# Mamba block with an FP4 feed-forward on one core: TensorE sums all sixteen products of a unit

## Chip, cores, metric

The kernel runs on one core of one Trainium2 chip. The metric is the device time of one execution in microseconds (us); less is better. Engines carry the names of the profile: PE is TensorE's matmul, PEld its weight load, DVE is VectorE, ACT is ScalarE, POOL is GpSimd, SP is SyncE.

## What is computed

An input of 16 sequences of 1024 tokens with 256 features goes through two residual layers, all in f32. The first is a state space layer with 4 heads of 128 channels, the second a gated feed-forward layer of width 704 whose activations and weights are rounded to blocks of FP4. The part that the change touches is the readout of the state space layer:

```
def step(s, inp):
    d_t, u_t, B_t, C_t = inp
    dA = jnp.exp(d_t[..., None] * A)
    s = s * dA + (d_t * u_t)[..., None] * B_t[:, :, None, :]
    y_t = jnp.einsum('bhdn,bhn->bhd', s, C_t)
    return (s, y_t)
```

The state has 16 entries n for each channel. y_t is the sum over these 16 of state times C.

## The kernel before

**Units and steps.** A unit is 512 tokens of one head; there are 128 units. A unit has 16 steps, one for each state entry n. At step n VectorE scans the 512 tokens of entry n in one instruction (L888), after it has multiplied the next entry's input term in PSUM (L878). Units 0 to 3 of each group of 8 are the first halves of a sequence for the four heads ("early" units here), units 4 to 7 the second halves ("late" units). After the last scan of an early unit VectorE copies the last column of the 16 states into carry (L893), which the late unit's scans start from. There is no such copy in a late unit.

**Readout.** Entries are taken in pairs p = 0 to 7. For a pair GpSimd multiplies two states with two rows of C into one of the four slots of prod (L619, 128 x 1024). For the pairs in the tuple ADDED, which are 0, 2, 4 and 6, GpSimd then adds the two halves of that slot (L623, 128 x 512). TensorE sums the products of a unit into the PSUM tensor ybank with an identity matrix as weights (L951, in sum_up): one f32 matmul of 512 columns for an added pair, two for any other. So a unit has 12 of these matmuls. Each f32 matmul shows in the profile as two records, its two passes. When the eighth pair is in, VectorE takes ybank into yg (L749).

**The order of the work is written out by hand.** Each engine has a function step(b, j, n) that is unrolled for the 8 units of a batch and 16 steps each; the batches 1 to 14 are a loop, the first and the last are peeled, with 8 units of lead and 8 of trail. The other work of both layers is laid into these steps: timetable gives for each job its unit, and due(job, slot) is true at the step slot mod 16. Each engine takes its instructions strictly in the order written, and semaphores join the engines.

**TensorE's order in one step n:** the input term db for step n + 2 (L939; it needs the scan of step n - 1), then at even n the sum of one pair (pair (n - 4) / 2 modulo 8: pair 0 at step 4, pair 2 at step 8, pair 4 at step 12, pair 6 at step 0 of the next unit), then the side work of that step. The side work that is spoken of later: at step 3 and at step 8 the up projection of the feed-forward tile in two halves (L1011), at steps 2 and 5 the gate projection (L1044), at steps 6 and 7 the input projection into pbank, at steps 12 and 13 that into bank_c (all L961), at steps 9 to 12 the down projection (L1058), at step 4 the dt projection (L989), at steps 14 and 15 the output projection (L1081), at step 0 the first bf16 residual (L981) and transposes of hh (L1025).

**VectorE's order in one step n:** L878 for step n + 1, then the jobs of between, the scan L888, then the jobs of behind. In step 9 between holds L820 for the second half (hh times bank_b, the result of L1011). In step 13 behind holds L840 (ot from bank_a, the result of L1058). In step 0 behind holds L835 (x from bank_a, the result of L1081). In step 3 between holds L749.

**GpSimd's order in one step n:** at even n the product of pair (n - 2) / 2 and, for a pair in ADDED, the addition; then the other jobs of that step. At step 14 these are pair 6 and L667, a multiplication of the 128 x 704 tile hh. At step 6 they are pair 2 and L634, and L487 on ScalarE waits for L634.

The first of the four slots of prod also serve, before unit 0, as scratch for the scales of the weights that are quantised then (w_scale).

Of the kernel before, what the change touches and what calls it, by code (L numbers as in the profile page):

```python
# [60 lines left out]
PAIRS = NST // 2  # L61
# [1 line left out]
P_RING = 4  # L63


ADDED = (0, 2, 4, 6)
START = {"norm": 6, "pre": 2, "scan": 0, "post": -4}
COUNT = {"norm": TILES, "pre": UNITS, "scan": UNITS, "post": TILES}
LEAD, TRAIL = 8, 8
# [26 lines left out]
def wait(eng, sem, value):  # L96

    if isinstance(value, int) and value <= 0:
        return
    eng.wait_ge(sem, value)  # L100
# [15 lines left out]
def build(nc, hidden, win_t, conv_w, conv_b, xw, dtw, dt_b, a_log, dskip, wo_t, w_gate, w_up, w_down,  # L116
# [4 lines left out]
    with ExitStack() as ctx:  # L121
# [6 lines left out]
        def sem(name):  # L128
            return ctx.enter_context(nc.semaphore(name))
# [82 lines left out]
        quantised = [sem(f"quantised_{w}") for w in ("gate", "up", "down")]  # L212
# [382 lines left out]
        def _(pool):  # L595
# [17 lines left out]
            def weigh(w, p):  # L613

                c, r = p % C_RING, p % P_RING
                wait(pool, scanned, w.val(NST, 2 * p + 2))
                wait(pool, c_landed[c], w.val(16 * PAIRS // C_RING, 16 * (p // C_RING + 1)))
                wait(pool, summed, w.val(PAIRS, p + 1 - P_RING))
                pool.tensor_tensor(prod[:, r, :, :], state[:, 2 * p:2 * p + 2, :], cs[:, c, :, :],  # L619
                                   ALU.mult).then_inc(weighted, 1)  # L620
                if p in ADDED:
                    wait(pool, weighted, w.val(PAIRS, p + 1))
                    pool.tensor_tensor(prod[:, r, 0, :], prod[:, r, 0, :], prod[:, r, 1, :],  # L623
                                       ALU.add).then_inc(added, 1)

            def step(b, j, n):
                u, due = timetable(b, j, n)
                if n % 2 == 0:
                    w = u if n else u + -1
                    if w.within(UNITS):  # L630
                        weigh(w, (n - 2) // 2 % PAIRS)
# [285 lines left out]
        def _(pe):  # L917
# [3 lines left out]
            def step(b, j, n):  # L921
                u, due = timetable(b, j, n)
                g = Ix(b, j * NST + n + 2, TRIP)
                gu, gn = g.k // NST, g.k % NST
                if g.within(STEPS):
                    spread_b(b, g)
                if n % 2 == 0:
                    w = u + (n - 4) // NST
                    if w.within(UNITS):
                        sum_up(w, (n - 4) // 2 % PAIRS)  # L930
                side(b, u, due)
# [10 lines left out]
            def sum_up(w, p):  # L942

                if p == 0:
                    wait(pe, y_taken, w.val())
                if p in ADDED:
                    wait(pe, added, w.val(len(ADDED), ADDED.index(p) + 1))
                else:
                    wait(pe, weighted, w.val(PAIRS, p + 1))
                for k in range(1 if p in ADDED else 2):  # L950
                    last = pe.matmul(ybank[:, :], ident[:, :], prod[:, p % P_RING, k, :],  # L951
                                     start=(p == 0), stop=(p == PAIRS - 1 and k == 1))
                last.then_inc(summed, 1)

            def side(b, u, due):
# [235 lines left out]
```

## Time and profile before

| | |
|---|---|
| three runs | 5384.91, 5389.06 and 5390.25 us, median 5389.06 |
| the profiled execution | 5384.97 us |
| its span, first to last instruction | 5382.9 us |
| VectorE busy | 5186.5 us, 96% |
| GpSimd busy | 4395.8 us, 82% |
| TensorE busy | 4155.3 us, 77% |
| ScalarE busy | 3306.0 us, 61% |
| mean granted TensorE clock | 0.959 |

Busy time is the time in which an engine's instructions ran; the granted clock is 1.00 at 2.4 GHz and 0.50 at 1.2 GHz, and a value between them in a stretch is a mix of the two. The time of an engine that is not the bound costs nothing while others hide it; so what matters here is where VectorE waits, and how much time lies between a result of another engine and VectorE's use of it.

### The profile page before, as it was taken

The numbers are of one execution on the slowest core, as the hardware profiler recorded it, in microseconds if no ns is written. First come the engines' busy times: TensorE is split into PE (matmuls) and PEld (weight loads), VectorE is DVE, ScalarE is ACT, GpSimd is POOL, SyncE is SP. The second block draws the span as 40 slices with busy tenths as digits, with TensorE's granted clock in tenths as the row PEclk, the third lists the DMA queues.
The fourth block names the chain that finished last, engine by engine and source line by source line (L and its number), as shares of the span: only waits on it lengthen the run. The fifth ranks groups of instructions, "written<-read, shape, count | busy, mean of one in ns | idle before, by whom it ended". The sixth has DMA issues, their size and how long they took to land.

```text
span 5382.9 us, 77607 instructions
## 1 busy us (share of the span) xinstructions
PE 4155.3 (77%) x12609; PEld 2142.2 (40%) x12844; DVE 5186.5 (96%) x7901; ACT 3306.0 (61%) x5776; POOL 4395.8 (82%) x3089
## 2 busy tenths in 40 slices
PE   4678777777777777777777777777777777777778
PEld 1234434444443444434344344443444434344444
DVE  6999999999999999999999999999999999999997
ACT  4666666666666666666666666666666666666663
POOL 5888888888888888888888888888888888888885
PEclk8999999999999999999999999999999999999999
DMA  2333333333333333333333333333333333333331
GB/s 93 134 116 115 114 112 112 115 115 115 109 116 111 116 114 114 115 112 115 113 113 111 115 112 114 111 118 112 112 114 113 116 110 117 112 112 114 114 113 45
DMA packets 211343, 602.12 MB, mean 112 GB/s; under 512 B 25446, under 2 KB 76774, under 8 KB 210790
## 3 DMA queue, kind: packets, MB, share of 16 engines
q1 hardware_dynamic: 209088, 594.30, 32.9%
q14 instruction: 415, 3.40, 0.2%
q8 instruction: 138, 2.26, 0.2%
q10 hardware_dynamic: 1702, 2.16, 0.2%
HBM read 575.39 MB, written 20.97 MB: 111 GB/s over the span
## 4 chain that ended last, share of the span: by engine, by line
DVE 42%; issue 20%; PE 16%; ACT 7%; POOL 6%; DVEq 3%; ACTq 1%; POOLq 0%; another core or an unknown queue 0%
DVE state L888 18%; DVE db L878 8%; PE ybank L951 7%; ACT decay L445 4%; DVE pbank L827 3%; DVEq L100 3%; PE bank_c L961 2%; POOL prod L619 2%; DVE hh L812 2%; DVE hw L803 2%; PE db L939 2%; PE bank_a L1058 1%; DVE hs L698 1%; DVE hh L820 1%; ACT sg L473 1%
## 5 line engine op out<-in xcount | busy, mean ns | idle before, releaser
L619 POOL TENSOR_TENSOR prod<-state,cs 128x1024 f32<-128x1024 f32 x1024 | 2415.3, 2359 | 799.2 <-DVE state L888 759.5
L445 ACT ACTIVATE decay<-delta,aneg 128x512 f32<-128x512 f32 x2048 | 1449.7, 720 | 1342.7 <-DVE state L888 1305.4
L951 PE MATMUL ybank<-prod,ident 128*128 128x512 f32 x3072 | 1568.4, 621 | 95.7 <-DVE state L888 89.5
L939 PE MATMUL db<-pieces,sel 128*128 128x512 bf16 x1844 | 719.5, 391 | 1015.9 <-DVE state L888 982.3
L878 DVE TENSOR_TENSOR db<-db,du 128x512 f32<-128x512 f32 x2048 | 1414.3, 691 | 69.4 <-issue 37.9
L888 DVE TENSOR_TENSOR_SCAN state<-decay,carry,db 128x512 f32<-128x512 f32 x1024 | 1297.4, 1267 | 0.0
L888 DVE TENSOR_TENSOR_SCAN state<-decay,db 128x512 f32<-128x512 f32 x1024 | 1234.9, 1206 | 0.0
L939 PEld LDWEIGHTS db<-pieces,sel 128*128 128x128 bf16 x2048 | 200.4, 98 | 1722.3 <-DVE state L888 1587.4
L951 PEld LDWEIGHTS ybank<-prod,ident 128*128 128x128 f32 x3072 | 564.8, 194 | 317.5 <-issue 264.0
L623 POOL TENSOR_TENSOR prod<-prod 128x512 f32<-128x512 f32 x512 | 650.0, 1270 | 40.1
L1058 PE MATMUL bank_a<-wd,ht 128*128 128x256 f32 x1536 | 446.1, 404 | 17.7 <-DVE state L888 15.7
L1058 PEld LDWEIGHTS bank_a<-wd,ht 128*128 128x128 f32 x1536 | 322.0, 210 | 200.0 <-issue 166.7
L1044 PE MATMUL bank_a<-wg,vt 128*128 128x352 f32 x1024 | 352.0, 467 | 15.6 <-DVE state L888 10.5
L1011 PE MATMUL bank_b<-wu,vt 128*128 128x352 f32 x1024 | 344.7, 459 | 0.7
L961 PE MATMUL bank_c<-xnt,win 128*128 128x512 f32 x512 | 328.2, 730 | 5.5 <-DVE spe L774 4.7
L961 PE MATMUL pbank<-xnt,win 128*128 128x512 f32 x512 | 264.9, 600 | 2.1 <-ACT spr L550 1.4
L1081 PE MATMUL bank_a<-wo,yg 128*128 128x256 f32 x1024 | 262.3, 379 | 2.0 <-DVE ot L840 1.1
L1011 PEld LDWEIGHTS bank_b<-wu,vt 128*128 128x128 f32 x1024 | 194.6, 190 | 142.5 <-issue 82.2
L1081 PEld LDWEIGHTS bank_a<-wo,yg 128*128 128x128 f32 x1024 | 194.2, 190 | 116.2 <-issue 99.3
L1044 PEld LDWEIGHTS bank_a<-wg,vt 128*128 128x128 f32 x1024 | 186.5, 196 | 73.2 <-issue 9.8
L535 ACT ACTIVATE hi<-pbank 128x512 bf16<-128x512 f32 x128 | 76.4, 597 | 204.8 <-PE pbank L1087 204.8
L430 ACT ACTIVATE xnt<-bank_b 128x256 f32<-128x256 f32 x128 | 49.1, 383 | 242.4 <-PE bank_b L1000 242.4
(125 smaller groups left out, 6436.3 us busy)
## 6 DMA issues: line engine op xcount, KB each, us to landing
cs<-c_rows SPq DMA_DIRECT2D x1024, 512.0 KB, 3.6
xin<-in_hidden SPq DMA_DIRECT2D x128, 128.0 KB, 3.8
xres<-in_hidden SPq DMA_DIRECT2D x128, 128.0 KB, 3.1
out_x<-ot SPq DMA_DIRECT2D x128, 128.0 KB, 3.6
c_rows<-xdbl SPq DMA_DIRECT2D x128, 32.0 KB, 3.6
win<-in_win_t SPq DMA_DIRECT2D x1, 1024.0 KB, 10.3
state<-in_w_gate ACTq DMA_DIRECT2D x1, 704.0 KB
state<-in_w_up ACTq DMA_DIRECT2D x1, 704.0 KB
```

Of the source, the lines that this page charges most:

```text
L445: act.activation(decay[:, g.k % RING, :], delta[:, gu % 2, :], ACT.Exp, scale=aneg[:, gu % HEADS, gn:gn + 1]).then_inc(decayed, 1)
L619: pool.tensor_tensor(prod[:, r, :, :], state[:, 2 * p:2 * p + 2, :], cs[:, c, :, :], ALU.mult).then_inc(weighted, 1)
L623: pool.tensor_tensor(prod[:, r, 0, :], prod[:, r, 0, :], prod[:, r, 1, :], ALU.add).then_inc(added, 1)
L878: dve.tensor_tensor(t[:, :], t[:, :], du[:, gu % 2, :], ALU.mult).then_inc(db_done, 1)
L888: dve.tensor_tensor_scan(state[:, n, :], decay[:, n % RING, :], db[DB_BANK[g.k % TRIP]][:, :], start, ALU.mult, ALU.add).then_inc(scanned, 1)
L939: pe.matmul(db[DB_BANK[g.k % TRIP]][:, :], sel[:, gn, :], pieces[:, gu % 2, :], start=True, stop=True).then_inc(b_spread, 1)
L951: last = pe.matmul(ybank[:, :], ident[:, :], prod[:, p % P_RING, k, :], start=(p == 0), stop=(p == PAIRS - 1 and k == 1))
L961: return pe.matmul((pbank, bank_c)[part][:, :], win[:, k, part * DI + h * P:part * DI + (h + 1) * P], xnt[:, v.mod(8) // 4, k, :], start=( ...
L1011: last = pe.matmul(bank_b[:, 0:HALF], vt[:, k, :], wu[:, k, part * HALF:(part + 1) * HALF], start=(k == 0), stop=(k == KM - 1))
L1044: last = pe.matmul(bank_a[:, 0:HALF], vt[:, k, :], wg[:, k, part * HALF:(part + 1) * HALF], start=(k == 0), stop=(k == KM - 1))
L1058: last = pe.matmul(bank_a[:, 0:DM], ht[:, k, :], wd[:, k, :], start=(k == 0), stop=(k == KI - 1))
L1081: last = pe.matmul(bank_a[:, 0:DM], yg[:, t.mod(8) // 4, h, i * P:(i + 1) * P], wo[:, h, :], start=(h == 0), stop=(h == HEADS - 1))
```

## The change

ADDED becomes empty. So L623 is never issued (512 instructions on GpSimd), and TensorE sums both halves of every pair (16 matmuls of 512 columns per unit in place of 12). For the pairs 0, 2, 4 and 6 TensorE now waits for the product (weighted) and no more for the addition (added). The accumulation is cleared by the first matmul of pair 0 alone. GpSimd gets one wait more, before the product of pair 1 of unit 0: that the three weights are quantised, since that product overwrites scales.

```
-ADDED = (0, 2, 4, 6)
+ADDED = ()
@@ weigh, on GpSimd
                 wait(pool, summed, w.val(PAIRS, p + 1 - P_RING))
+                if p == 1 and isinstance(w.b, int) and w.val() == 0:
+                    for done in quantised:
+                        pool.wait_ge(done, 10)
                 pool.tensor_tensor(prod[:, r, :, :], state[:, 2 * p:2 * p + 2, :], cs[:, c, :, :],
                                    ALU.mult).then_inc(weighted, 1)
@@ sum_up, on TensorE
                 for k in range(1 if p in ADDED else 2):
                     last = pe.matmul(ybank[:, :], ident[:, :], prod[:, p % P_RING, k, :],
-                                     start=(p == 0), stop=(p == PAIRS - 1 and k == 1))
+                                     start=(p == 0 and k == 0), stop=(p == PAIRS - 1 and k == 1))
                 last.then_inc(summed, 1)
```

## Rows read from the trace of the kernel before

**Rows 1.** The profile's page, part 1: busy time, share and instructions.

```profile
PE 4155.3 (77%) x12609; PEld 2142.2 (40%) x12844; DVE 5186.5 (96%) x7901; ACT 3306.0 (61%) x5776; POOL 4395.8 (82%) x3089
```

**Rows 2.** Waits of VectorE: us in total, times, longest; then those in the tail.

```profile
DVE ot L840 <- PE bank_a L1058: 33.3, 76, 5.3
DVE yg L749 <- PE ybank L951: 24.5, 29, 3.9
...
DVE ot L840 <- PE bank_a L1058: 10.1, 8, 5.3
...
DVE yg L749 <- PE ybank L951: 3.9, 1, 3.9
```

**Rows 3.** Groups by line: busy us, mean ns | idle before, releaser.

```profile
L623 POOL TENSOR_TENSOR prod<-prod 128x512 f32<-128x512 f32 x512 | 650.0, 1270 | 40.1
L893 DVE COPY carry<-state 128x16 f32<-128x16 f32 x64 | 44.8, 700 | 2.2
```

**Rows 4.** Timeline, TensorE: start, us, instruction; a pair of one matmul, one of two.

```profile
2582.71 1.02 PE L951 MATMUL ybank<-prod,ident 128*128 128x512 f32 x2
...
2606.89 1.88 PE L951 MATMUL ybank<-prod,ident 128*128 128x512 f32 x4
```

**Rows 5.** Windows, steps 5 to 9 of an early unit: length, busy PE, PEld, DVE, ACT, POOL, clock.

```profile
2727.68:2730.47 2.79, 1.57 (x5) 0.80 (x5) 2.79 (x7) 1.87 (x3) 2.60 (x3) 1.00 0.49 186
2730.47:2732.43 1.96, 1.90 (x5) 0.99 (x6) 1.96 (x7) 1.59 (x3) 1.70 (x1) 1.00 0.01 2
2732.43:2734.14 1.71, 1.71 (x6) 0.67 (x4) 1.71 (x4) 1.66 (x2) 1.63 (x2) 1.00 0.08 14
2734.14:2736.28 2.14, 2.14 (x7) 1.18 (x7) 2.14 (x4) 1.46 (x5) 2.14 (x3) 1.00 0.72 232
2736.28:2738.93 2.65, 1.14 (x4) 0.48 (x3) 2.57 (x5) 2.62 (x4) 1.74 (x3) 1.00 0.20 76
```

**Rows 6.** Timeline of steps 8 and 9 of that unit, all engines, up to L820.

```profile
2733.17 1.26 POOL L623 TENSOR_TENSOR prod<-prod 128x512 f32<-128x512 f32 x1
...
2734.40 0.38 PE L939 MATMUL db<-pieces,sel 128*128 128x512 bf16 x1
...
2734.62 1.02 PE L951 MATMUL ybank<-prod,ident 128*128 128x512 f32 x2
...
2735.48 1.35 PE L1011 MATMUL bank_b<-wu,vt 128*128 128x352 f32 x4
...
2736.18 0.69 DVE L878 TENSOR_TENSOR db<-db,du 128x512 f32<-128x512 f32 x1
...
2736.95 0.52 DVE L820 TENSOR_TENSOR hh<-hh,bank_b 128x352 f32<-128x352 f32 x1
```

**Rows 7.** Timeline, the same place in a late unit.

```profile
2900.73 1.35 PE L1011 MATMUL bank_b<-wu,vt 128*128 128x352 f32 x4
...
2902.20 0.52 DVE L820 TENSOR_TENSOR hh<-hh,bank_b 128x352 f32<-128x352 f32 x1
```

**Rows 8.** Windows, step 12 of a late unit, TensorE near half clock.

```profile
2911.48:2913.59 2.11, 2.05 (x4) 1.02 (x5) 2.11 (x6) 0.99 (x2) 1.86 (x1) 0.55 0.00 0
```

**Rows 9.** Timeline of that unit: TensorE at step 12's start, L840 in step 13.

```profile
2911.54 0.51 PE L939 MATMUL db<-pieces,sel 128*128 128x512 bf16 x1 [2.18 <-DVE state L888]
...
2916.33 0.42 DVE L840 TENSOR_TENSOR ot<-bank_a,x 128x256 f32<-128x256 f32 x1 [0.38 <-PE bank_a L1058]
```

**Rows 10.** Timeline, the same place at full clock, in another late unit.

```profile
2584.42 1.03 PE L1058 MATMUL bank_a<-wd,ht 128*128 128x256 f32 x4
...
2586.81 0.40 DVE L840 TENSOR_TENSOR ot<-bank_a,x 128x256 f32<-128x256 f32 x1
```

**Rows 11.** Timeline around the copy L893: GpSimd and VectorE; last row: early in the run.

```profile
2753.17 1.26 POOL L623 TENSOR_TENSOR prod<-prod 128x512 f32<-128x512 f32 x1
2754.39 1.39 POOL L667 TENSOR_TENSOR hh<-hh,hs 128x704 f32<-128x704 f32 x1
...
2754.85 0.96 DVE L893 COPY carry<-state 128x16 f32<-128x16 f32 x1
...
126.95 0.17 DVE L893 COPY carry<-state 128x16 f32<-128x16 f32 x1
```

**Rows 12.** Timeline of steps 1 to 3 of one unit: TensorE and L749.

```profile
2760.63 0.39 PE L939 MATMUL db<-pieces,sel 128*128 128x512 bf16 x1 [2.41 <-DVE state L888]
2760.85 2.98 PE L951 MATMUL ybank<-prod,ident 128*128 128x512 f32 x4
...
2763.98 0.75 DVE L749 SCALAR_TENSOR_TENSOR yg<-uu,dsk,ybank 128x512 f32<-128x512 f32 x1 [0.62 <-PE ybank L951]
```

More of the change, by code:

```diff
@@ L63 @@
 P_RING = 4
-ADDED = (0, 2, 4, 6)
+ADDED = ()
 START = {"norm": 6, "pre": 2, "scan": 0, "post": -4}
@@ L618, in weigh @@
                 wait(pool, summed, w.val(PAIRS, p + 1 - P_RING))
+                if p == 1 and isinstance(w.b, int) and w.val() == 0:
+                    for done in quantised:
+                        pool.wait_ge(done, 10)
                 pool.tensor_tensor(prod[:, r, :, :], state[:, 2 * p:2 * p + 2, :], cs[:, c, :, :],
@@ L951, in sum_up @@
                     last = pe.matmul(ybank[:, :], ident[:, :], prod[:, p % P_RING, k, :],
-                                     start=(p == 0), stop=(p == PAIRS - 1 and k == 1))
+                                     start=(p == 0 and k == 0), stop=(p == PAIRS - 1 and k == 1))
                 last.then_inc(summed, 1)
```

## The prediction

> **What bounds the kernel now.** The page's busy times come first [rows 1]: VectorE is busy in 5186.5 of 5382.9 us, 96%, GpSimd in 82% and TensorE in 77%. Taking 650 us of additions [rows 3] off GpSimd can therefore give little by itself: the sum of VectorE's own instructions stays. What the change can move is of two kinds: VectorE's waits for others, and VectorE instructions whose own length depends on GpSimd. The waits of VectorE [rows 2] show that nearly all it waits for is TensorE: 33.3 us before L840 and 24.5 us before L749, of which 10.1 and 3.9 us lie in the tail behind the last scan. A total of waits doesn't tell how close the others are to waiting. So the timeline has to be read at each place where VectorE takes a TensorE result that comes behind an enlarged pair sum in TensorE's written order.
>
> **What one more matmul costs.** A pair of one matmul stands as 1.02 us of two passes, a pair of two as 1.88 us of four [rows 4]. The difference, 1.88 - 1.02 = 0.86 us, is what each of the 512 new matmuls takes of TensorE's queue at full clock. That is 440 us in all, and TensorE would be about 85% busy: not the bound on the average, but its work is in order, and it comes in lumps at steps 4, 8, 12 and 0.
>
> **Step 8 (pair 2), the main term.** In steps 6, 7 and 8 TensorE has no spare time: it is busy 1.90 of 1.96, 1.71 of 1.71 and 2.14 of 2.14 us [rows 5]. In step 8 it issues db, the pair's matmul and then the second half of the up projection, L1011, which L820 waits for in step 9, ahead of the scan. In the early unit L1011 starts at 2735.48 and L820 at 2736.95, 1.47 us later, though the L878 ahead of L820 ended at 2736.87 [rows 6]. In the late unit it is 2900.73 and 2902.20, again 1.47 us [rows 7]. Two starts at the same distance from the producer mean that there is no slack: L820 starts when the result is there. So the new 0.86 us shows in full on VectorE, in every unit in which a tile is in the feed-forward layer. L820's slot 41 is reached by the tiles in units 6 to 127, 122 times: 122 x 0.86 = 105 us; a little slack where L820 now starts unhindered takes 2 off: **+103 us**. Behind the stall nothing is queued on VectorE that could run in its place, and the scan of step 9, the product of the next pair, and TensorE's next db all wait with it. TensorE's 1.51 us of idle time in step 9 [rows 5] comes after L1011 and is of no use for it.
>
> **Step 12 (pair 4).** Here the down projection is behind the pair, and L840 takes it after scan 13. Two cases stand in the trace. Where TensorE sat idle for 2.18 us before step 12 and its clock then fell to a mean of 0.55 in that step [rows 8, 9], L840 already waits 0.38 us. Where the clock stays full, the four passes of L1058 start at 2584.42 and last 1.03 us, to 2585.45; L840 starts at 2586.81 [rows 10], so there are about 1.3 us of slack, and 0.86 fits. In the units of the first case the wait rises to about 0.34 + 0.86 = 1.20 us. There are 76 - 8 = 68 of them now, with 33.3 - 10.1 = 23.2 us [rows 2], 0.34 on average. How many there will be can't be read off: the place of the fall moves as units get longer, and they get longer by unlike amounts. I take 45 as an estimate, between 20 and 80: 45 x 1.20 - 23.2 = **+31 us** (bounds +1 and +73).
>
> **Step 0 (pair 6) and step 4 (pair 0).** Behind pair 0 stand the dt projection and, in step 5, the gate projection; step 5 has 2.79 - 1.57 = 1.22 us of TensorE idle [rows 5], which covers 0.86. If that cover were gone, step 6, which has none, would pass it on to L820, 0.86 us a unit. Behind pair 6 are transposes and the residual; step 1 ends with TensorE idle for 2.41 us [rows 12]. Taken as nothing. In late units at full clock the pair of step 12 leaves TensorE 0.86 us later at db in step 15; I put 5 us on this, an estimate between 0 and 25 us.
>
> **The copy L893, a gain.** This instruction of 16 elements takes 0.17 us early in the run and 0.96 us in the unit shown; there L667 on GpSimd starts before it and ends at 2755.78, 0.03 us ahead of the copy's end at 2755.81 [rows 11]. So a GpSimd instruction already under way holds it up. L667 stands right behind the addition of pair 6. Without that addition it starts 1.27 us earlier [rows 3] and ends at 2754.5, before the copy begins at 2754.85. All 64 copies then take 0.17 us: 44.8 - 64 x 0.17 = **-34 us** (bounds -34 and 0, if other GpSimd work slides into the gap). The Trainium skill, page "SBUF — State Buffer" (section "Who interferes with whom"), says that a copy of VectorE in a mode that uses both ports and a GpSimd instruction shut each other out, and that the one issued second waits for the end of the first; by it the gain would be the same, and the two lengths of L893 agree with it.
>
> **L749, a gain.** The 24.5 us before it [rows 2] come from passes at low clock after the idle time of step 1: four passes last 2.98 us instead of 1.88 after 2.41 us idle, and L749 waits 0.62 us [rows 12]. The 0.86 us of pair 6, and the lateness from step 12, fill most of that idle time. Of the 20.6 us ahead of the tail I take **-15 us** (0 to -21).
>
> **The rest.** The waits for the products in place of the additions are shorter. The new GpSimd wait is for quantisation that lies before unit 0, at no cost. ScalarE's chain behind L634 starts earlier, and VectorE does not wait for it.
>
> **Sum.** 103 + 31 + 5 - 34 - 15 = +90 us on the profiled execution's 5385.0 us: 5475 us. The median of the three runs is 4 us above that execution, so 5475 to 5479; I predict 5478 us, 1.7% slower.
>
> **The rivals.**
> - *The busier TensorE keeps its clock.* The fall at step 12 goes too, and with it L840's waits of 23.2 us: 5389 + 103 - 23 - 34 - 21 + 5 = 5419 us. For it: there is more work in each unit. Against it: none of the new matmuls lies in steps 9 to 11, where the idle time before the fall is, and VectorE's stall in step 9 doesn't shorten it. The Trainium skill, page "TensorE: Matmul & The Clock Gate" (section "What's actually happening"), says that the throttled state is the default and that activity releases it; by that rule more activity favours this rival. Chance 0.15.
> - *The low clock comes in most units and the late lumps add up.* 80 units at 1.20 us, the step 0 and 15 terms at 25, the gains on the copy and on L749 halved: 5389 + 103 + 73 + 25 - 17 - 8 = 5565 us at the far end, 5530 in the middle of this case. Chance 0.12.
> - *Faster: pair 2 is now held up by its addition.* If TensorE at step 8 stood waiting for L623, the second matmul would only fill that wait, and L1011 would not move. It decides once the addition ends 0.86 us or more after TensorE is ready for the pair. Then 5389 - 34 - 15 - 10 = 5330 us. Against it: the addition ends at 2734.43, and the pair's matmul starts 0.22 us after db's at 2734.40 [rows 6], which is db's own length in the queue. Chance 0.06.
> - *It cancels.* L1011 takes part of the 0.86 us from slack in units other than the two shown, and the gains balance the rest: within 0.2% of before. Chance 0.04.
>
> **How the numbers follow.** The forecast as described, about 5440 to 5510, has 0.63. The range takes in most of the first two rivals: 5415 to 5535. A change of 0.2% (11 us) is about what a measurement of this kernel can tell from none. Faster by more: 0.06; within: 0.04; slower by more: 0.90.
>
> **What the profile after would show.** L951 with 4096 records instead of 3072 and no L623. L820 with about 100 us of wait for L1011; if it is near 0, the main term is wrong. L840 waiting about 1.2 us where the clock is low. L893 at 0.17 us on average. L749's wait down to a few us. VectorE's busy time down by 34 us and the span up. What would make the prediction wrong: slack before L820 in most units, or a clock that falls at other places than now.

## The result, and the profile after

The changed kernel takes 5423.62 us (median of five runs, 5421.93 to 5426.27), the kernel before 5390.25 us (five runs, 5384.91 to 5400.97). The ratio is 1.0060, with a 95% interval from 1.0045 to 1.0074: 33 us slower. The forecast was 5478 us: right in sign, and the measured time is inside its range, but the forecast loss of 88 us is 2.6 times the measured one. Between the two profiled executions the spans differ by 5422.4 - 5382.9 = 39.5 us; the steps below are held against that number.

From the page after, the busy times, two groups and (from the answer by line, which keeps shapes apart) the copy. The lines of the changed kernel are numbered 3 higher behind the edit in weigh: L823 is L820 of before, L843 is L840, L752 is L749, L896 is L893, L1014 is L1011, L954 is L951, L881 is L878, L1061 is L1058. In the kernels of the experiments the numbers move by a few lines more; the names stay: hh waits for bank_b, ot for bank_a, yg for ybank, and db is the input term of the scans. The columns of the table below name the lines of before.

```profile
PE 4437.0 (82%) x13868; PEld 2297.8 (42%) x13868; DVE 5143.5 (95%) x7901; ACT 3324.7 (61%) x5776; POOL 3760.1 (69%) x2577
...
L954 PE MATMUL ybank<-prod,ident 128*128 128x512 f32 x4096 | 1979.8, 607 | 1.0 <-POOL prod L622 1.0
...
L823 DVE TENSOR_TENSOR hh<-hh,bank_b 128x352 f32<-128x352 f32 x256 | 130.0, 508 | 105.9 <-PE bank_b L1014 105.4
...
L896 DVE COPY carry<-state 128x16 f32<-128x16 f32 x64 | 11.3, 176 | 2.2
```

L951's 3072 records are 4096 now, L623 is gone, GpSimd fell from 82% to 69% busy [rows 1], and VectorE's busy time fell by 43 us while the span grew. The copy went from 44.8 to 11.3 us [rows 3]. The waits of VectorE after (us in total, times, longest), against rows 2:

```profile
DVE hh L823 <- PE bank_b L1014: 105.4, 129, 0.9
DVE ot L843 <- PE bank_a L1061: 40.1, 33, 5.3
...
DVE yg L752 <- PE ybank L954: 2.7, 1, 2.7
```

The first line is new and carries the loss. In the timeline of step 8 of an early unit the pair has four passes and the up projection comes behind them:

```profile
1478.07 1.88 PE L954 MATMUL ybank<-prod,ident 128*128 128x512 f32 x4
...
1479.79 1.35 PE L1014 MATMUL bank_b<-wu,vt 128*128 128x352 f32 x4
...
1481.26 0.52 DVE L823 TENSOR_TENSOR hh<-hh,bank_b 128x352 f32<-128x352 f32 x1 [0.94 <-PE bank_b L1014]
```

L823 starts 1.47 us after L1014, the distance that stood there before [rows 6, 7]. The granted clock rose from a mean of 0.959 to 0.986. Steps 12 and 13 of three units in a row after (length, busy time of each engine, then the clock, the DMA share and GB/s) show how it falls now, in one unit and not in its neighbours:

```profile
1449.85:1454.24 4.39, 4.34 (x14) 2.44 (x15) 4.39 (x8) 2.12 (x4) 3.60 (x2) 1.00 0.16 60
1490.36:1494.75 4.39, 4.34 (x7) 2.07 (x8) 4.39 (x7) 2.11 (x4) 3.58 (x2) 0.63 0.16 37
1532.15:1536.55 4.40, 4.34 (x14) 2.45 (x15) 4.40 (x9) 2.12 (x4) 3.58 (x2) 1.00 0.16 55
```

A "low unit" below is one of the units 8 to 119 (112 units) in whose steps 11 to 13 the clock's records show half clock for more than 0.3 us. Before there are 67 of them, and 45 of these are followed by another; after there are 23, and none is followed by another. The waits of L840 hang on them: in units 0 to 124, every one of its waits is in a unit whose clock is low in steps 11 to 13 (67 waits before, 24 after, 85 in e3_late2 below).

### The profile page after: what moved, and what is told of

It reads as the page before. It is cut to its first block and busy times, and to the rows that moved or that the text cites. A ratio compares the mean times of both kernels' runs of the same rounds, so it can differ in the third digit from the quotient of the medians.

```text
span 5422.4 us, 78931 instructions
## 1 busy us (share of the span) xinstructions
PE 4437.0 (82%) x13868; PEld 2297.8 (42%) x13868; DVE 5143.5 (95%) x7901; ACT 3324.7 (61%) x5776; POOL 3760.1 (69%) x2577
## 5 line engine op out<-in xcount | busy, mean ns | idle before, releaser
L954 PE MATMUL ybank<-prod,ident 128*128 128x512 f32 x4096 | 1979.8, 607 | 1.0 <-POOL prod L622 1.0
L942 PE MATMUL db<-pieces,sel 128*128 128x512 bf16 x2048 | 791.2, 387 | 904.6 <-DVE state L891 876.8
L881 DVE TENSOR_TENSOR db<-db,du 128x512 f32<-128x512 f32 x2048 | 1400.9, 684 | 69.9 <-issue 36.8
L954 PEld LDWEIGHTS ybank<-prod,ident 128*128 128x128 f32 x4096 | 766.7, 194 | 557.8 <-issue 512.5
L1061 PE MATMUL bank_a<-wd,ht 128*128 128x256 f32 x1536 | 412.6, 379 | 1.3 <-ACT ht L479 1.2
L1061 PEld LDWEIGHTS bank_a<-wd,ht 128*128 128x128 f32 x1536 | 292.0, 191 | 164.4 <-issue 142.1
L1014 PE MATMUL bank_b<-wu,vt 128*128 128x352 f32 x1024 | 344.7, 459 | 0.0
L964 PE MATMUL bank_c<-xnt,win 128*128 128x512 f32 x512 | 266.9, 604 | 4.7 <-DVE spe L777 4.7
L656 POOL TENSOR_TENSOR delta<-spl,spe 128x512 f32<-128x512 f32 x128 | 163.2, 1275 | 135.2 <-DVE spe L777 135.1
L1014 PEld LDWEIGHTS bank_b<-wu,vt 128*128 128x128 f32 x1024 | 194.6, 190 | 142.4 <-issue 82.5
L479 ACT ACTIVATE ht<-bank_b 128x384 f32<-128x384 f32 x256 | 123.6, 483 | 182.2 <-PE bank_b L1028 182.0
L823 DVE TENSOR_TENSOR hh<-hh,bank_b 128x352 f32<-128x352 f32 x256 | 130.0, 508 | 105.9 <-PE bank_b L1014 105.4
```

Of the source, the lines that this page charges most:

```text
L656: pool.tensor_tensor(delta[:, v.mod(2), :], spl[:, :], spe[:, :], ALU.subtract).then_inc(sp_pool, 1)
L881: dve.tensor_tensor(t[:, :], t[:, :], du[:, gu % 2, :], ALU.mult).then_inc(db_done, 1)
L942: pe.matmul(db[DB_BANK[g.k % TRIP]][:, :], sel[:, gn, :], pieces[:, gu % 2, :], start=True, stop=True).then_inc(b_spread, 1)
L964: return pe.matmul((pbank, bank_c)[part][:, :], win[:, k, part * DI + h * P:part * DI + (h + 1) * P], xnt[:, v.mod(8) // 4, k, :], start=( ...
L1014: last = pe.matmul(bank_b[:, 0:HALF], vt[:, k, :], wu[:, k, part * HALF:(part + 1) * HALF], start=(k == 0), stop=(k == KM - 1))
L1061: last = pe.matmul(bank_a[:, 0:DM], ht[:, k, :], wd[:, k, :], start=(k == 0), stop=(k == KI - 1))
```

## Experiments

Ratios are to runs of the kernel before on the same chip, with 95% intervals. The waits include the tail, where L840 and its counterparts wait in 8 places, 10.1 us in total (11.7 to 11.8 us in e1_pair6, e3_late2, e4_late24 and e8_after_warm). Each kernel has one profile, so the columns behind the ratio are of one execution. The mean granted clock is known for every run and varies little between runs of one kernel: 0.952 to 0.964 before, 0.986 in all five of the changed kernel, 0.965 to 0.969 in e3_late2, 0.979 to 0.980 in e5_late2_delay.

| kernel | time, us | ratio | wait of L820 | wait of L840 | wait of L749 | L893, busy | low units (followed by one) |
|---|---|---|---|---|---|---|---|
| before | 5390 | 1 | 1 | 33 | 24.5 | 44.8 | 67 (45) |
| changed | 5424 | 1.0060 | 105 | 40 | 2.7 | 11.3 | 23 (0) |
| e1_pair6 | 5335 | 0.9906 | 1 | 33 | 2.7 | 11.3 | 69 (46) |
| e2_pair2 | 5462 | 1.0140 | 105 | 26 | 22 | 41.4 | 43 (20) |
| e3_late2 | 5390 | 1.0007 | 1 | 119 | 2.7 | 11.2 | 82 (58) |
| e4_late24 | 5377 | 0.9984 | 1 | 12 | 2.7 | 11.3 | 76 (50) |
| e5_late2_delay | 5429 | 1.0066 | 1 | 65 | 2.7 | 11.3 | 42 (4) |
| e6_late2_warm | 5269 | 0.9770 | 1 | 10 | 2.7 | 11.2 | 0 |
| e7_pair6_warm | 5295 | 0.9821 | 1 | 10 | 2.7 | 11.3 | 0 |
| e8_after_warm | 5388 | 0.9992 | 105 | 12 | 2.7 | 11.3 | 0 |
| e9_late24_warm | 5268 | 0.9780 | 1 | 10 | 2.7 | 11.3 | 0 |
| e10_added6 | 5482 | 1.0176 | 106 | 50 | 12 | 41.2 | 29 (9) |
| e11_before_warm | 5421 | 1.0064 | 1 | 10 | 76 | 57.2 | 0 |

### One pair at a time

**e1_pair6** against the changed kernel:

```
-ADDED = ()
+ADDED = (0, 2, 4)
```

> Only pair 6 loses its addition (ADDED is 0, 2, 4); pairs 0, 2 and 4 are as before. Theory (the place in TensorE's order decides): no new matmul lies ahead of L820's or L840's producer, so L820 does not wait and L840 waits about as before (60 to 75 units, 20 to 27 us ahead of the tail). L893 falls from 44.8 to about 11 us, since nothing stands ahead of L667 but the product; L749's wait falls by 10 to 22 us, since step 1's idle time shrinks. Time about 54 us under before: 5336 us, 5325 to 5350. Rival A (it is the busier TensorE that keeps its clock, wherever the work is): the units at low clock at steps 11 to 13 fall well below 60 and L840's waits with them, 5320 us. Rival B (L893 is held up by something other than the addition ahead of L667): L893 stays near 700 ns, time 5365 to 5375 us.

Measured: 5335.07 us, ratio 0.9906 (0.9887 to 0.9924). Its waits and its copy:

```profile
DVE ot L843 <- PE bank_a L1061: 32.7, 69, 7.0
...
DVE yg L752 <- PE ybank L954: 2.7, 1, 2.7
...
L896 DVE COPY carry<-state 128x16 f32<-128x16 f32 x64 | 11.3, 176 | 2.2
```

Both gains are those of pair 6 alone: the copy 33.5 us, L749's wait 21.8 us. L840's wait and the number of low units are as before. There is one small loss: L704 (a scaling of 44 values, L701 of before) takes 226 ns on average, 188 before.

```profile
L704 DVE TENSOR_SCALAR hs<-hs 128x44 f32<-128x44 f32 x128 | 29.0, 226 | 0.2
```

In the traces of this kernel and of before, a GpSimd instruction is under way at its start in 113 of 128 places, and in these it takes 234 ns on average here, 190 before. So giving up one addition is worth 52 us, and giving up all four costs 33.

**e2_pair2** against the changed kernel:

```
-ADDED = ()
+ADDED = (0, 4, 6)
```

> Only pair 2 loses its addition (ADDED is 0, 4, 6). Theory: the new matmul of step 8 is ahead of L1011, L820 waits 0.8 to 0.94 us in some 120 units, 95 to 105 us. L893 and L749 stay as before (about 45 us and 24 us of wait). L840 waits only where the clock is low, 0.4 us each. Time about 100 us over before, 5490 us, 5475 to 5505. Rival A (busier TensorE keeps its clock): one matmul more per unit, units at low clock clearly fewer, time 5465 to 5475 us. Rival C (the waits of L820 come from all four new matmuls together, by a backlog): L820 waits under 50 us, time under 5440 us.

Measured: 5461.94 us, ratio 1.0140 (1.0120 to 1.0159), 75 us over before and not 100.

```profile
DVE hh L823 <- PE bank_b L1014: 105.5, 129, 0.9
...
DVE ot L843 <- PE bank_a L1061: 25.7, 51, 5.3
DVE yg L752 <- PE ybank L954: 22.3, 22, 3.2
```

The whole wait before L823 is pair 2's alone; a backlog of all four (rival C) is out. The 25 us by which the time falls short of 100 are smaller items, all less than before: L840's waits 7.6, the idle time before L878 8, the scans 4, the copy 3, L749 2. The low units fell from 67 to 43, so they change even where the other pairs are untouched. That fits rival A as well as a matter of timing; the next kernels tell them apart.

### Where TensorE issues pair 2, and what then becomes late

**e3_late2**: pair 2 behind the side work of step 8.

```
+LATE = (8,)
@@ step, on TensorE
-                if n % 2 == 0:
-                    w = u + (n - 4) // NST
-                    if w.within(UNITS):
-                        sum_up(w, (n - 4) // 2 % PAIRS)
+                w = u + (n - 4) // NST
+                if n % 2 == 0 and n not in LATE and w.within(UNITS):
+                    sum_up(w, (n - 4) // 2 % PAIRS)
                 side(b, u, due)
+                if n in LATE and w.within(UNITS):
+                    sum_up(w, (n - 4) // 2 % PAIRS)
```

> The changed kernel, with one edit: in step 8 TensorE issues the two matmuls of pair 2 behind the side work (L1014, the up projection), not ahead of it. The work is the same. Theory: L1014 now comes even earlier than before the change, L823's wait of 105 us goes to about 1 us, and the two matmuls of pair 2 run in step 9, where TensorE is idle for 1.5 us. The gains stay (L896 at 0.17 us, L752 without waits). Time 5424 - 100 = about 5323 us, 5310 to 5340. Rival (the wait moves on: the pair's matmuls delay db or the down projection of the next steps): L881 or L843 wait more, and under half of the 100 us comes back, over 5370 us.

Measured: 5390.49 us, ratio 1.0007 (0.9993 to 1.0020). The wait before the up projection's reader is gone, and the expectation still failed, for the other wait grew:

```profile
DVE ot L844 <- PE bank_a L1063: 118.7, 94, 6.9
DVE db L882 <- PE db L944: 32.8, 65, 2.6
```

The rival of the expectation got the size right and the reason wrong. Pair 2's matmuls run in step 9's idle time and make no wait of L844 longer: ahead of the tail a wait of L844 is (118.7 - 11.7) / 86 = 1.24 us, where it was 1.20 in the changed kernel. There are 86 of them in place of 25. The work is that of the changed kernel, yet low units rose from 23 to 82. Three units in a row, steps 12 and 13:

```profile
1115.71:1120.10 4.39, 4.33 (x7) 1.95 (x8) 4.39 (x8) 2.11 (x4) 3.59 (x2) 0.63 0.16 62
1156.60:1160.99 4.39, 4.33 (x7) 1.89 (x8) 4.39 (x8) 2.11 (x4) 3.58 (x2) 0.64 0.17 44
1197.49:1201.88 4.39, 4.33 (x7) 1.80 (x8) 4.39 (x7) 2.11 (x4) 3.59 (x2) 0.65 0.16 62
```

**e4_late24**: pair 4 too is behind the side work of its step 12.

```
-LATE = (8,)
+LATE = (8, 12)
```

> As e3_late2, and in step 12 too the two matmuls of pair 4 are issued behind the side work (down projection, L1061). TensorE's work is again that of the changed kernel. Theory on the clock (a unit at low clock grows by L843's wait of 1.2 us, which moves the next unit out of the place where the clock falls; where that wait is gone, low units come in runs again): L843 waits under 12 us with the tail's 10 us, but units at low clock rise from 25 to 45 or more. Time 5323 - 25 = about 5300 us, 5285 to 5320. Rival A (the busier TensorE keeps its clock): same work, so units at low clock stay at 25 or fewer; the time is about the same 5300 us, the two differ in the count.

Measured: 5377.34 us, ratio 0.9984 (0.9974 to 0.9993), against an expected 5300.

```profile
DVE db L882 <- PE db L944: 147.5, 194, 2.2
...
DVE ot L844 <- PE bank_a L1063: 11.7, 8, 6.9
```

L844's 107 us ahead of the tail went, and 115 us more of waits came before db, which now stands behind pair 4. The wait moved to the next result in TensorE's order. With the same work on TensorE, rival A had 25 low units or fewer; there are 76, 50 of them followed by another, and rival A is out. The theory on timing had the count, but not by its reason. Its reason was that a low unit no longer grows once this wait is gone. But the wait came back before db, and a low unit is still longer than the others (medians of 41.5 and 39.9 us from step 11 to step 11), as in e3_late2 (41.5 and 39.7), and in both low units come in runs. That L843's wait is what broke up the runs in the changed kernel is not shown.

**e5_late2_delay**: e3_late2 with 0.8 us more for VectorE in step 9, and nothing changed on TensorE. Left out of the cut are the tile junk and a wait for ident ahead of the first unit.

```
@@ between, on VectorE
+                if n == 9 and Ix(b, j * NST + n, TRIP).within(STEPS):
+                    dve.tensor_reduce(junk[:, j % 2, :, :], ident[:, :].rearrange("p (n k) -> p n k", k=BLK)
+                                      .unsqueeze(1).broadcast_to([P, 5, 8, BLK]), AX, ALU.max)
```

> The kernel e3_late2 (TensorE's pair 2 behind the up projection) with one instruction more on VectorE in step 9 of each unit, a reduction of a constant that takes about 0.8 us and whose result nobody reads; TensorE's work is unchanged. It puts the changed kernel's stall of step 9 back without its cause. Theory 1 (timing decides where the clock falls: a stretch at low clock recurs in the next unit or not by how long the unit is): units at low clock fall from 82 of 112 to under 45, L844's kind of wait from 119 us to under 60, and the time is 5390 + 102 - 65 = about 5425 us, 5405 to 5445. Theory 2 (only TensorE's work decides): units at low clock stay at 75 or more and the time is 5390 + 102 = 5490 us or more.

Measured: 5429.13 us, ratio 1.0066 (1.0049 to 1.0083).

```profile
L746 DVE TENSOR_REDUCE junk<-ident 128x40 f32<-128x640 f32 x128 | 104.3, 815 | 0.0
...
DVE ot L848 <- PE bank_a L1068: 64.6, 53, 5.3
```

VectorE got 93 us more to do (815 ns each, part of it under its neighbours), and the kernel grew by only 39 us: low units fell from 82 to 42, only 4 of them followed by another, and L840's counterpart waited 54 us less. So where TensorE's clock falls depends on when the units' idle stretches come, with TensorE's work unchanged. The wait of L823 puts about the same delay into the changed kernel. A delay of this kind can account for 40 of the 59 low units between e3_late2's 82 and the changed kernel's 23; the rest is open.

### The idle time before step 12

**e6_late2_warm, e7_pair6_warm, e8_after_warm, e11_before_warm, e9_late24_warm** add the same edit to e3_late2, e1_pair6, the changed kernel, the kernel before and e4_late24. At the end of step 11 TensorE repeats the db matmul for step 13 six times, into the same bank, and only the last tells VectorE:

```
+REPEATS = 6
@@ spread_b, on TensorE
-                pe.matmul(db[DB_BANK[g.k % TRIP]][:, :], sel[:, gn, :], pieces[:, gu % 2, :],
-                          start=True, stop=True).then_inc(b_spread, 1)
+                first = pe.matmul(db[DB_BANK[g.k % TRIP]][:, :], sel[:, gn, :], pieces[:, gu % 2, :],
+                                  start=True, stop=True)
+                if gn != 13:
+                    first.then_inc(b_spread, 1)
@@ step, on TensorE, behind the side work
+                if gn == 13 and g.within(STEPS):
+                    again(b, g)
```

Here again(b, g) issues that matmul REPEATS times with then_inc(b_spread, 1) on the last.

> The kernel e3_late2 with six repeats of the db matmul (the same input, the same output, 512 columns in bf16, about 0.21 us each) at the end of step 11, inside the 2.2 us in which TensorE is idle before step 12. Nothing of the result changes. If the low clock of steps 11 to 13 is what makes VectorE wait for L843's producer, and the idle time before step 12 is what lets the clock fall: units at low clock go under 10 of 112, that wait from 119 us to about 12 us (the tail), the time to 5390 - 107 = about 5283 us, 5270 to 5300. Rival (the wait is TensorE's amount of work in steps 12 and 13, not its clock): the wait stays over 80 us and the time over 5360 us.

Measured: 5268.75 us, ratio 0.9770 (0.9754 to 0.9786).

```profile
1523.92 1.46 PE L955 MATMUL db<-pieces,sel 128*128 128x512 bf16 x6
1526.42 0.39 PE L947 MATMUL db<-pieces,sel 128*128 128x512 bf16 x1 [1.05 <-DVE state L893]
...
DVE db L883 <- PE db L947: 17.7, 26, 2.1
DVE ot L845 <- PE bank_a L1075: 10.1, 8, 5.3
```

The idle time before step 12 is 1.05 us here, a median of 2.32 in e3_late2; no unit is low, L845 waits in the tail alone, and 122 us are gone from e3_late2. TensorE does more and the kernel is faster: the wait was the clock, not the work. It also confirms that pair 2's matmuls in step 9 delay nothing at full clock.

> The kernel e1_pair6 (only pair 6 without its addition) with the same six repeats at the end of step 11. Theory: L843's waits of 22 us ahead of the tail and part of the 17 us of waits for db go, the time falls from 5335 to about 5307 us, 5298 to 5320. Rival: as for e6_late2_warm, no change from 5335 us.

Measured: 5295.02 us, ratio 0.9821 (0.9805 to 0.9837), 12 us better than expected; VectorE's idle time before db fell by 11.5 us, from 72.7 to 61.2. Its wait for bank_a is the tail's alone:

```profile
DVE ot L844 <- PE bank_a L1073: 10.1, 8, 5.3
```

> The changed kernel with the same six repeats at the end of step 11. Theory: L823 goes on waiting for the up projection, 105 us, since the repeats are nowhere near step 8; L843's 30 us ahead of the tail go. Time 5424 - 30 = 5394 us, 5380 to 5405: still not faster than before. Rival (the clock is what makes L823 wait too): its wait falls under 60 us and the time under 5360 us.

Measured: 5388.27 us, ratio 0.9992 (0.9983 to 1.0002), as expected. 35 us come back with the clock, 28 of them in L840's waits, and the main term stays:

```profile
DVE hh L824 <- PE bank_b L1026: 105.4, 129, 0.9
...
DVE ot L844 <- PE bank_a L1073: 11.8, 8, 7.0
```

> The kernel before with the six repeats of the db matmul at the end of step 11 and nothing else. Theory: L840's 23 us of waits ahead of the tail go, and part of those for db, -28 us; but without a stall ahead of it the copy L893 meets L667 at its start in every early unit and goes from 44.8 to about 57 us, +12. L749 keeps its 20 us, for the idle time of step 1 is untouched. Time 5389 - 16 = about 5373 us, 5360 to 5385. Rival (the clock alone is worth what it was worth in e3_late2, over 60 us): 5330 us or less.

Measured: 5421.10 us, ratio 1.0064 (1.0044 to 1.0084): slower than before, where 5373 was expected.

```profile
DVE yg L750 <- PE ybank L963: 75.9, 66, 3.7
...
DVE ot L841 <- PE bank_a L1070: 10.1, 8, 5.3
...
L894 DVE COPY carry<-state 128x16 f32<-128x16 f32 x64 | 57.2, 894 | 2.2
```

Two parts came as expected: L840's wait went, and the copy grew by 12.4 us. L667 is under way at the start of 60 of the 64 copies in both kernels; the length of these 60 rose from a mean of 735 ns to 942. The third part was missed: L749 waits 51 us more. Without the low stretch at step 12 the clock falls after the next long idle time, that of step 1, and pair 7 runs at low clock:

```profile
1731.44:1735.87 4.43, 4.32 (x14) 2.43 (x15) 4.43 (x9) 2.11 (x4) 3.66 (x3) 1.00 0.17 47
...
1746.05 0.61 PE L942 MATMUL db<-pieces,sel 128*128 128x512 bf16 x1 [2.41 <-DVE state L889]
1746.45 3.35 PE L963 MATMUL ybank<-prod,ident 128*128 128x512 f32 x4
...
1749.95 0.75 DVE L750 SCALAR_TENSOR_TENSOR yg<-uu,dsk,ybank 128x512 f32<-128x512 f32 x1 [1.16 <-PE ybank L963]
```

The clock is low in steps 1 to 3 in 57 of 112 units, and in each of these L750 waits; before it was 32 units. In the kernels in which pair 6 has its second matmul that idle time is shorter. Its median is 2.38 us here, 0.98 in e6_late2_warm and 1.72 in e7_pair6_warm, where 4 units and 1 unit are low in these steps. So there the repeats cost nothing at step 1. A row of e6_late2_warm at the same place:

```profile
1539.99 0.39 PE L947 MATMUL db<-pieces,sel 128*128 128x512 bf16 x1 [0.91 <-DVE state L893]
```

> The kernel e4_late24 (pairs 2 and 4 behind the side work of their steps) with the six repeats of the db matmul at the end of step 11. If the 148 us in which L881 waits for db in e4_late24 are also the low clock of steps 12 and 13, they fall to about 20 us at full clock, and the time is that of e6_late2_warm, 5269 us within 8. If it is the order (pair 4's matmuls ahead of the next step's db), over 60 us of that wait stay and the time is over 5320 us.

Measured: 5268.38 us, ratio 0.9780 (0.9760 to 0.9799), the same as e6_late2_warm within 0.4 us. At full clock pair 4's place in step 12 doesn't matter; of the 148 us of e4_late24, 132 were the clock too.

```profile
DVE db L883 <- PE db L947: 15.7, 24, 2.2
```

### Pair 6's addition put back

**e10_added6**: the changed kernel with pair 6's addition alone put back.

```
-ADDED = ()
+ADDED = (6,)
```

> The changed kernel with the addition of pair 6 alone put back on GpSimd (ADDED is 6): TensorE has one matmul of 512 columns less in step 0. Theory: L893 is held up again by L667, which stands behind that addition, and goes from 11 us back to 30 to 45 us in total; L823 keeps its 105 us of wait. L752: if pair 6's own matmul is what fills the idle time of step 1, its wait comes back to 10 to 24 us; if the lateness left over from step 12 does it too, it stays under 8 us. Time 5424 + 30 + 12 = about 5463 us, 5445 to 5480. Rival (the gain on L893 came with the change as a whole): L893 stays near 11 us, 5435 us or less.

Measured: 5481.71 us, ratio 1.0176 (1.0155 to 1.0196), 58 us over the changed kernel.

```profile
DVE ot L843 <- PE bank_a L1061: 49.6, 40, 5.3
...
DVE yg L752 <- PE ybank L954: 11.7, 18, 3.6
...
L896 DVE COPY carry<-state 128x16 f32<-128x16 f32 x64 | 41.2, 644 | 2.2
```

The copy is held up again (41.2 us), so the addition ahead of L667 is its cause. L749's wait comes back by 9 us of 22. TensorE's idle time in step 1 (median) goes from 0.91 us to 1.77, where it was 1.99 before, and the clock is low in steps 1 to 3 in 14 units, where it was none in the changed kernel and 32 before. That lateness left over from step 12 keeps the rest of the wait away is likely and not shown. The time is 19 us over the expectation and 2 us over its range: there are 32 waits of L843 ahead of the tail in place of 25, 10 us, and the rest is spread. Pairs 0 and 4 were not changed by themselves in any run.

## Why the prediction was right in sign and wrong in size

- **The price of a matmul and the main term (step 8).** Right. 0.86 us per unit, no slack before L820: 103 us were forecast. The listed wait rose by 104 us, from 1.2 to 105.4, and gaps before hh too short to be listed shrank by 5, so 100 us came. e2_pair2 and e3_late2 put it on pair 2's place in the order.
- **Step 12.** This is the step that failed, by the number of units in which the wait comes. Its price was right: (40.1 - 10.1) / 25 = 1.20 us for each wait, as forecast. Its count was not: 25 waits, not 45, so +7 us and not +31. The forecast said that the place of the fall moves as units get longer and then took a number from the middle of 20 to 80, with no row behind it; 25 lies within its bounds. The runs show that a longer step 9 by itself takes low units away (82 to 42 in e5_late2_delay). It is the largest of the errors of size, and about half of the whole.
- **The copy L893.** Right: -33.5 us against -34, and e1_pair6 and e10_added6 tie it to the addition of pair 6. L667 was under way at the start of 60 of the 64 copies before, and of none after.
- **L749.** Right in kind, -22 us against -15: all of its wait ahead of the tail went, not most of it.
- **db in late units.** 5 us were forecast and next to nothing came: VectorE's idle time ahead of the product with db (L878) was 69.4 us before and is 69.9 after.
- **Left out of the sum.** VectorE's scans took 6 us less and L701 (188 to 162 ns) 3 us less; a GpSimd instruction is under way at its start in 113 of 128 places before and in 1 after. For the scans no cause was found.
- **Together.** 24 (count) + 3 (L820) + 7 (L749) + 5 (db) + 9 (left out) = 48 of the 90 - 39.5 = 50.5 us by which the sum was too high for the two profiled executions. Between the medians the change is 33.4 us and not 39.5: the profiled execution of before is about 5 us below the median of its five runs.
- **The rival nearest in time was wrong in its reason.** "The busier TensorE keeps its clock" had 5419 us. The low units did fall, from 67 to 23, but it also had L840's waits gone, and they grew from 33.3 to 40.1 us; that it came within 5 us of the time is luck. e3_late2 and e4_late24 do the changed kernel's work on TensorE with 82 and 76 low units. The Trainium skill, page "TensorE: Matmul & The Clock Gate" (section "What's actually happening"), says that activity releases the throttle. e6_late2_warm agrees with it: work put into the idle time before the fall removes it (82 low units to none). Work put elsewhere needn't.

Why a low unit recurs in some kernels and not in others is settled only so far: with TensorE's work the same the count went from 82 to 42 by VectorE's timing alone, and with the work of the changed kernel it was 23, 76 and 82 by the order alone. What rule would give 23 and not 42 stays open.

## What to carry to other kernels

An engine that is 77% busy and takes its work in a written order can have full steps, and one more instruction there can cost its whole length at the bound engine; read the distance from producer to reader in the timeline, because a wait total of 1 us can mean no slack at all. Place added work behind the result that someone waits for, and into the idle time ahead of a dense stretch. Judge the parts of such a change one by one: here one quarter of it is worth 52 us, another costs 75 (its wait alone is 105), and with the order and the idle time mended the whole of it gives 120 us (5269 against 5389). The repeats alone don't give this: without the change they cost 32 us.

## What the runs showed of the hardware that was not expected

- Six matmuls that compute nothing new, 1.46 us per unit, took 122 us off e3_late2 with the granted clock at a mean of 0.996 in place of 0.966; the same six made the kernel before 32 us slower, mostly since the fall moved from step 12 to step 2.
- A VectorE copy of 16 elements takes 0.18 us free and up to 0.96 us behind a GpSimd instruction that has started; a scaling of 44 elements has a mean of 160 ns where it starts free in the changed kernel and of 234 ns behind a GpSimd instruction in e1_pair6.
- A delay of 815 ns on VectorE in each unit cost 39 us in place of 93, through where TensorE's clock falls.
